# Expert choices of images 8 to 31 placed between the expert products, with fewer and wider casts of the score parts

## What is computed

```python
logits = jnp.einsum('bsd,ed->bse', x, gate_w)            # 64 experts
top_logits, indices = jax.lax.top_k(logits, 6)
scores = jax.nn.softmax(top_logits, axis=-1)
W_sel = lattice_weights[indices]                          # 64x64 each
xW = jnp.einsum('bsd,bskde->bske', x, W_sel)
lattice_out = jnp.einsum('bske,bsk->bse', xW, scores)
h = x + jnp.einsum('bsd,ed->bse', lattice_out, out_w) + out_b   # then a layernorm
```

## Time and profile before

| | us |
|---|---|
| median of 3 runs | 1178.67 (1178.66 to 1181.56) |
| the profiled execution | 1181.52 |
| its span, first to last instruction | 1179.7 |
| PE busy in it | 1075.1 (91%) |
| DVE, ACT, POOL busy | 625.6, 422.6, 125.5 |
| mean granted TensorE clock | 0.962 of full speed |

### The profile page before, as it was taken

The page is one execution under the profiler, slowest core; times in us unless marked ns, Lnnn a source line. Parts: engine busy times, 40 slices in busy tenths (PEclk is TensorE's granted clock), DMA queues, the critical chain, the costliest instruction groups (busy, mean ns, idle before and its releaser), DMA issues.

```text
span 1179.7 us, 34307 instructions
## 1 busy us (share of the span) xinstructions
PE 1075.1 (91%) x15860; PEld 715.5 (61%) x15860; DVE 625.6 (53%) x790; ACT 422.6 (36%) x588; POOL 125.5 (11%) x120
## 2 busy tenths in 40 slices
PE   5899999999999998999899999999998999349996
PEld 4578667767767533677677677767226888322221
DVE  2238445824834221358248446733153577857887
ACT  2332223133223485231332233223667786540000
POOL 6000000000000000000000000020012754242111
PEclk9999999999999899999999999999899999559998
DMA  5220130022022201300220130020001000000000
GB/s 179 86 72 2 50 97 13 2 86 72 3 71 76 83 6 63 82 19 2 86 72 2 64 88 8 2 93 9 13 15 38 2 1 2 1 1 1 5 5 10
DMA packets 25652, 46.62 MB, mean 40 GB/s; under 512 B 9437, under 2 KB 10488, under 8 KB 24869
## 3 DMA queue, kind: packets, MB, share of 16 engines
q1 hardware_dynamic: 24694, 43.49, 12.2%
q10 hardware_dynamic: 384, 0.66, 0.2%
q0 software_dynamic: 432, 0.29, 0.1%
HBM read 30.25 MB, written 10.89 MB: 35 GB/s over the span
## 4 chain that ended last, share of the span: by engine, by line
PE 77%; DVE 11%; ACT 4%; issue 2%; DMA 2%; SPq 1%; POOL 1%; ACTq 0%; POOLq 0%; DVEq 0%
PE PSALL L1198 22%; PE PSALL L1057 9%; PE PSALL L1166 7%; PE PSALL L1074 7%; PE PSALL L482 5%; DVE WORK L1390 5%; PE PSALL L1276 4%; PE PSALL L1189 4%; PE PSALL L1142 4%; PE PSALL L1286 3%; PE PSALL L470 2%; PE PSALL L387 2%; DMA WORK<-MIXED 2%; DVE WORK L1409 2%; PE PSALL L366 2%
## 5 line engine op out<-in xcount | busy, mean ns | idle before, releaser
L1409 DVE STREAM_TRANSPOSE WORK<-PSALL 128x1024 f32<-128x1024 f32 x128 | 152.4, 1229 | 320.2 <-PE PSALL L1166 320.2
L1198 PEld LDWEIGHTS PSALL<-EW,WORK 64*128 64x128 f32 x4096 | 251.5, 194 | 65.5 <-issue 48.3
L1198 PE MATMUL PSALL<-EW,WORK 64*128 64x128 f32 x4096 | 267.8, 284 | 12.8 <-DVE WORK L1409 12.8
L1326 ACT ACTIVATE X<-PSALL,TABLES 128x1024 f32<-128x1024 f32 x128 | 141.9, 1115 | 334.4 <-PE PSALL L1198 334.4
L1390 DVE STREAM_TRANSPOSE WORK<-PSALL 128x1024 f32<-128x1024 f32 x100 | 119.1, 1229 | 58.4 <-PE PSALL L1057 54.6
L1074 PE MATMUL PSALL<-TABLES,WORK 128*128 128x128 f32 x1000 | 138.9, 288 | 4.7 <-DVE WORK L1390 0.5
L1074 PEld LDWEIGHTS PSALL<-TABLES,WORK 128*128 128x128 f32 x1000 | 121.2, 195 | 32.7 <-issue 19.2
L1307 ACT COPY SPEC<-PSALL 128x400 f32<-128x400 f32 x64 | 53.7, 847 | 175.4 <-PE PSALL L1074 172.2
L1057 PE MATMUL PSALL<-WORK,DW 32*64 32x256 f32 x3200 | 103.4, 389 | 12.6 <-DMA B<-in_fc_b 12.6
L1386 DVE STREAM_TRANSPOSE WORK<-X 128x1024 f32<-128x1024 f32 x96 | 111.4, 1204 | 0.0
L932 DVE TENSOR_TENSOR WORK<-PSALL,X 128x832 f32<-128x832 f32 x80 | 80.7, 1021 | 19.7 <-PE PSALL L470 19.5
(11 more groups left out here) (145 smaller groups left out, 983.0 us busy)
## 6 DMA issues: line engine op xcount, KB each, us to landing
SW<-in_spec_w SPq DMA_DIRECT2D x160, 80.0 KB, 2.4
spec_scr<-MIXED SPq DMA_DIRECT2D x24, 400.0 KB, 3.3
SPEC<-spec_scr SPq DMA_DIRECT2D x32, 200.0 KB
WORK<-spec_scr SPq DMA_DIRECT2D x16, 200.0 KB
WORK<-MIXED SPq DMA_DIRECT2D x64, 40.0 KB
WORK<-in_coords_w SPq DMA_DIRECT2D x2, 1024.0 KB, 4.9
XC<-in_coords_c SPq DMA_DIRECT2D x2, 1024.0 KB, 7.1
hid_scr<-WORK SPq DMA_DIRECT2D x64, 8.0 KB
```

Of the source, the lines that this page charges most:

```text
L1198: m = pe.matmul(PS[2 * p + z][:, 2 * b * GRID:(2 * b + 2) * GRID], G[64 * z:64 * z + 64, n % 2, b, h:h + 4, :, c].rearrange("p q o -> p (q ...
L1326: nc.scalar.activation(X[:, n].rearrange("p b (z d) c w -> p d z b (c w)", z=2)[:, p, :, :, 2 * t * GRID:2 * (t + 1) * GRID], PSALL[:, 2 * ...
L1409: nc.vector.transpose(G[:, n % 2, 2 * x + y].rearrange("p h o v -> p o h v"), PSALL[:, 4 + 2 * x:6 + 2 * x, :].rearrange("p k (h o v) -> p ...
```

## The change

Only choice 0 (images 0 to 7) and the parts of chunks 0 and 1 stay in the step loop, which ends at i = 51. The gate rows of the last two chunks come at steps 48 and 50. Choices 1 to 3 start on DVE after the products of pairs 0, 10 and 20, one step per pair, and their remainders 10 and 12 pairs on; PE makes their score rows at pairs 9 and 11 on; ACT's exponentials and casts and POOL's products stand outside the step loop, in the order of the choices. The two halves of the experts share one instruction: one high cast of 96x520, one remainder and one middle cast of 64x520, one low part of 32x520. High, middle and low now lie in the third, second and first 32 rows. The score products are steps 7 and 8. `SC3` and the logits `LG` move to other memory, since `ZX` and `LT` of the experts lie where they were. POOL's two long additions follow the last low part as before. The six matmuls at L337, whose result nothing reads, are there in both kernels.

```diff
-TAIL_STEPS = PARTS_AT + LB * (LK - 1) + 7
+TAIL_STEPS = 52
+CHOICE_PAIR = [None, 0, 10, 20]
+def rows_step(i):
+    if i <= ROWS_AT + 5 * BC:
+        return (i - ROWS_AT) // BC if i >= ROWS_AT and (i - ROWS_AT) % BC == 0 else None
+    return 6 + (i - ROWS_AT - 22) // 2 if i in (ROWS_AT + 22, ROWS_AT + 24) else None
...
-        LG = modes_mem[0:TOK, NT:NT + NIMG * LW].rearrange("p (b e) -> p b e", b=NIMG)
+        LG = arena[0:TOK, 14272:14272 + NIMG * LW].rearrange("p (b e) -> p b e", b=NIMG)
...
-               for m in (modes_mem[0:TOK, 0:LB * 6 * EH], arena[0:TOK, 14432:14432 + LB * 6 * EH])]
+               for m in (arena[0:TOK, 10272:10272 + LB * 6 * EH], arena[0:TOK, 12352:12352 + LB * 6 * EH])]
...
     PE, score_rows
-                for g in range(2):
-                    pe.wait_ge(sc_ready, c * BC // LB + 1)
-                    if c:
-                        pe.wait_ge(rest_ready, 2 * c - 1 + g)
-                    transposes(c, lambda b: SC3[b // LB % 2][:, b % LB, g]..., 3 * EH, PS[6 + g], st_full)
+                pe.wait_ge(sc_ready, 2 * (c * BC // LB + 1))
+                if c:
+                    pe.wait_ge(rest_ready, c)
+                for i in range(BC):
+                    b = c * BC + i
+                    for g in range(2):
+                        m = pe.transpose(PS[6 + g][0:3 * EH, i * TOK:(i + 1) * TOK], SC3[b // LB % 2][:, b % LB, g]...)
+                m.then_inc(st_full, 1)
...
     PE, expert loop
+                for k in range(1, LK):
+                    if n // 2 - CHOICE_PAIR[k] in (9, 11):
+                        score_rows(2 * k + (n // 2 - CHOICE_PAIR[k]) // 11)
...
     ACT
-                for g in range(2):
-                    act.wait_ge(st_full, 2 * c + g + 1)
-                    nc.scalar.copy(PARTS3[g][0:3 * EH, c * CT:(c + 1) * CT], PS[6 + g][0:3 * EH, 0:CT]).then_inc(high_ready, 1)
+                act.wait_ge(st_full, c + 1)
+                nc.scalar.copy(PARTS3[0:3 * EH, :, t], PSALL[0:3 * EH, 6:8, 0:CT]).then_inc(high_ready, 1)
...
-                for g in range(2):
-                    act.wait_ge(rest_ready, 2 * c + g + 1)
-                    for r in (EH, 2 * EH):
-                        m = nc.scalar.copy(PARTS3[g][r:r + EH, ...], REST[g][r:r + EH, ...])
-                    m.then_inc(mid_ready, 1)
+                act.wait_ge(rest_ready, c + 1)
+                nc.scalar.copy(PARTS3[0:2 * EH, :, t], REST[0:2 * EH, :, t]).then_inc(mid_ready, 1)
...
+            exp_logits(1)
             for z in range(NZ):
+                for k in ([1], [2, 3])[z] if z < 2 else []:
+                    high_part(2 * k)
+                    middle_part(2 * k)
+                    high_part(2 * k + 1)
+                    if k + 1 < LK:
+                        exp_logits(k + 1)
+                    middle_part(2 * k + 1)
...
     POOL
+                nc.gpsimd.tensor_tensor(PARTS3[0:EH, :, t], REST[0:EH, :, t], PARTS3[0:EH, :, t], ALU.subtract).then_inc(lo_ready, 1)
...
+            for k in range(1, LK):
+                chosen_scores(k)
+                low_part(2 * k)
+                low_part(2 * k + 1)
...
     DVE, expert loop, after each product L932
+                    for k in range(1, LK):
+                        step = n // 2 - CHOICE_PAIR[k]
+                        if 0 <= step <= 8:
+                            choice(k, step)
+                        if step in (10, 12):
+                            rest(2 * k + step // 12)
```

More of the change, by code:

```diff
@@ L449, in tail_tensor @@
                     turn_attended((i - LAG - 2) // BC)
[L450 to L457, removed]
+                if rows_step(i - 1) is not None:
+                    gate_logits(rows_step(i - 1))
+                if rows_step(i) is not None:
+                    gate_rows(rows_step(i))
+                if i in (PARTS_AT, PARTS_AT + 2):
+                    score_rows((i - PARTS_AT) // 2)
             pe.wait_ge(gt_ready, NC)
@@ L489, in output_projection @@
                 if c == 0:
[L490 removed]
+                    pe.wait_ge(rest_ready, NC)
                 if c >= 2:
@@ L603, in tail_scalar @@
                     deviation(1, (i - LN_STEP - 7) // LB)
[L604 to L615, removed]
-            for z in range(NZ):
+                if rows_step(i - 1) is not None:
+                    gate_logits_out(rows_step(i - 1))
+                if rows_step(i) is not None:
+                    gate_rows_out(rows_step(i))
+                if i == CHOICE_AT + 2:
+                    exp_logits(0)
+                if i in (PARTS_AT, PARTS_AT + 2):
+                    high_part((i - PARTS_AT) // 2)
+                if i in (PARTS_AT + 3, PARTS_AT + 5):
+                    middle_part((i - PARTS_AT) // 4)
+            exp_logits(1)
+            for z in range(NZ):
+                for k in ([1], [2, 3])[z] if z < 2 else []:
[5 more added lines that the diff above has]
+                    middle_part(2 * k + 1)
                 if z >= 2:
@@ L647, in tail_pool @@
             for g in range(2):
-                nc.gpsimd.memset(PARTS3[g][3 * EH:128], 0.0).then_inc(zeros_set, 1)
+                nc.gpsimd.memset(PARTS3[3 * EH:128, g], 0.0).then_inc(zeros_set, 1)
                 pool.wait_ge(zeros_set, g + 1)
@@ L676, in low_part @@
             def low_part(c):
[L677 to L681, removed]
+                pool.wait_ge(weighed, c // 2 + 1)
+                t = slice(c * CT, (c + 1) * CT)
+                pool.wait_ge(mid_ready, c + 1)
+                nc.gpsimd.tensor_tensor(PARTS3[0:EH, :, t], REST[0:EH, :, t], PARTS3[0:EH, :, t], ALU.subtract).then_inc(lo_ready, 1)
             pool.wait_ge(nv_ready, NC)
@@ L707, in tail_pool @@
                     square(1, (i - LN_STEP - 3) // LB)
[L708 to L713, removed]
+                if i == CHOICE_AT + 5:
+                    chosen_scores(0)
+                if i in (PARTS_AT + 4, PARTS_AT + 6):
+                    low_part((i - PARTS_AT) // 6)
+            for k in range(1, LK):
+                chosen_scores(k)
+                low_part(2 * k)
+                low_part(2 * k + 1)
+            pool.wait_ge(lo_ready, NC)
             whole = [TOK, NIMG, GRID]
@@ L840, in choice @@
                         link(nc.vector.reciprocal(st[:, 3, a], st[:, 0, a]))
[L841 removed]
+                    if step in (7, 8):
                         if k >= 2:
[L843 to L848, removed]
+                            dve.wait_ge(st_full, LB // BC * (k - 1))
+                        g, thrice = step - 7, [TOK, LB, 3, EH]
+                        nc.vector.tensor_tensor(SC3[k % 2][:, :, g], SC[:, a, g * EH:(g + 1) * EH].unsqueeze(2).broadcast_to(thrice),
+                                                st[:, 3, a].unsqueeze(2).unsqueeze(3).broadcast_to(thrice), ALU.mult).then_inc(sc_ready, 1)
                 def rest(c):
                     t = slice(c * CT, (c + 1) * CT)
[L852 to L855, removed]
+                    dve.wait_ge(high_ready, c + 1)
+                    nc.vector.tensor_tensor(REST[0:2 * EH, :, t], PSALL[0:2 * EH, 6:8, 0:CT], PARTS3[0:2 * EH, :, t], ALU.subtract
+                                            ).then_inc(rest_ready, 1)
                 for i in range(TAIL_STEPS):
[L858 to L860 removed]
                     if i < NIMG:
@@ L902, in tail @@
                                                     ).then_inc(half_ready if step == 1 else y_ready, 1)
[L903 to L908, removed]
+                    if i == CHOICE_AT - 1:
+                        dve.wait_ge(ho_out.sem, PASSES * ho_out.stride)
+                        link(nc.vector.memset(LG[:, :, EXPERTS:LW], SENTINEL))
+                    if CHOICE_AT <= i <= CHOICE_AT + 8:
+                        choice(0, i - CHOICE_AT)
+                    if i in (PARTS_AT + 2, PARTS_AT + 4):
+                        rest((i - PARTS_AT) // 4)
                 def add_projection(c):
```

18 lines of the change are left out of this document (10 added, 8 removed).

## The result

The kernel after takes 1165.26 us (median of 4 runs, 1163.19 to 1167.91) against 1178.66 (4 runs, 1177.11 to 1181.56): ratio 0.9903, 95% interval 0.9874 to 0.9932. The profiled execution took 1165.57 us, its span is 1163.8. Timed again (6 runs, beside 11 of the kernel before) it gave 1166.65 against 1176.02, ratio 0.9930 (0.9903 to 0.9957). Forecast were 1171.7 and a gain of 7.0 us; the gain is 13.4 us by the first set and 9.4 by the second.

A forecast was written before the change was run, and what follows sets the result against it. Ahead of the experts a chain hopping between engines, none full, was taken as the bound, then PE in the experts. -27.8 + 14.2 + 2.6 + 4.0 = -7.0 us takes the median from 1178.67 to 1171.7; range 1165 to 1181.

The forecast's parts named there:

- Start of the experts, -27.8: Chain ahead of the experts: with three choices gone from it, the first expert product comes at 1026.4 against 1054.2 us.
- Pairs 0 to 32, +14.2: Expert pairs with choice steps on DVE's queue: DVE becomes the bound, 59.0 us against 44.8, a loss of 14.2.
- the added 1.7: Pairs 0 to 32: 1.7 us for half clock at the start, waits after score products and a meeting with POOL.
- POOL's additions, +2.6: POOL's two long additions move behind pair 32; DVE waits 3.7 us and PE loses about 2.6.
- PE runs on for about one pair of its ring: During DVE's wait for POOL after product 37, PE keeps working about one pair, so it loses about 2.6 us.
- the bound of 3.7: Upper bound of the loss from POOL's additions: DVE's whole wait after product 37, 3.7 us.
- TensorE's clock, +4.0: Pairs 0 to 32: two or three falls of PE's clock, costing 4 us.
- The crowded pairs should cost a fall each: Pairs 10 to 12 and 20 to 22, PE about 60% busy: each a clock fall of about 6 us.
- The sum without the clock: Whole change without the clock term: -27.8 for the start, +14.2 for the pairs, +2.6 for POOL's additions.
- Rival 1: Clock holds in pairs 0 to 32, PE's gaps under 1 us each; the 4 us fall away, 1167.7; chance 0.22.
- Rivals 2 and 3: Pairs 0 to 32: clock at each level half the time, 1176.7, chance 0.18; clock stays 0.50, 1194, chance 0.12.

The follow-up runs named there:

- the run with the held low parts: Kernel after with POOL's last residual shift started after choice 1's subtraction, and low parts of chunks 0 and 1 held until DVE's normalizations are done: 1159.89 us.
- the narrow run: Kernel after with two high casts, four middle casts, two remainders and two low parts per chunk again: 1170.27 us, ratio 0.9940.
- the padded one: Kernel after with one unused DVE maximum over 65x512 behind each of products 0 to 31; products 0 to 33 took 77.86 us, single profiled run.
- the run with only the wide casts: Kernel after with all four choices back ahead of the experts, wide casts, joined remainders and low parts kept: 1175.69 us against 1176.86, ratio 0.9993.

## Why the prediction was right

The time lies in the range and the direction is right; the mechanism was as forecast: experts early, DVE the bound for 33 pairs, POOL's additions uncovered. By its steps:

- **Start of the experts, -27.8.** Measured 41.94 to 14.68, -27.3 (with product 0, -27.4). The middle cast, 0.62 us, was priced at 0.60. Missing was that POOL's low parts would hold up DVE's normalizations (3.05 us for two, PE idle 1.40), which the run with the held low parts puts at 0.9.
- **Pairs 0 to 32, +14.2.** Measured +12.6. The sum of DVE's instructions was 57.3 and the stretch took 57.43, but that they meet is partly luck: DVE was busy 55.2 us of it and idle 2.2. Waits of about the size of the added 1.7 were there, and the terms for the instructions, taken from start to start, were 2 too high.
- **POOL's additions, +2.6.** Measured +3.9, and 4.4 by the run that moves one of them away. The step that failed is "PE runs on for about one pair of its ring": the bound of 3.7, the whole wait, was nearly the price. PE, the bound from there on, gets nothing back; it idled 3.11 us in one piece and then ran at half clock for 3 us in one execution and some 7 in the other.
- **TensorE's clock, +4.0.** Measured 0. This is the term that was mis-sized, and the reason that the gain is larger than forecast. "The crowded pairs should cost a fall each" failed twice. At 2.49 us of work in 4 the clock held in both crowded places (from 1044 and from 1062), and it held from product 2 to product 33 in seven of the eight profiles with this stretch unpadded; and a fall costs little there, half a microsecond or less in the narrow run and 1.4 to 3.6 us for three in the padded one, because DVE has the longer queue. I carried the fall in the earlier trace rows over from a place with other matmuls.
- **The sum without the clock**, -11.0, lies near the -10.75 of the trace because three smaller errors nearly cancel: the start gained 0.5 less, the pairs lost 1.6 less, POOL's additions cost 1.3 more. That closeness is luck too.
- Rival 1 (the clock holds) is what happened, although PE's gaps were not all under 1 us, as it had them: they go up to 1.28. Rivals 2 and 3 need a half clock over much of the stretch; no run had that with the stretch unpadded, so their prices stay untested. The rule of the Trainium skill (TensorE: Matmul & The Clock Gate, "A second HAM failure mode: psum-queue depth-cycling") that short idles between groups of matmuls can make the clock go back and forth isn't borne out by the kernel after, where gaps of 0.15 to 1.28 us at 43.87 us of work in 54 left the clock at 1.00. In the padded run, where PE had 1.37 us of work in 4, it went down and up three times, as the page says.
- The rest of the 13.4 us in the medians, some 2.2, is not shown to belong to the change. In the later sets the kernel before had medians of 1176.86 (23 runs), 1176.02 and 1175.64 (11 each), so the first set's 1178.66 lay high; the second pair of timings is 9.4 us apart, and the change is worth 10.2 to 11.2 by the traces, the 0.4 in front included.

What stays open: why the clock fell in one run after PE had worked 2.58 of 4 us and held in another after 2.49 of 4. Nothing here tells these two apart. Nor is it shown where the 0.4 us ahead of the score rows come from; the run with only the wide casts has them too (14.92).

## What to carry to other kernels

A chain of short steps that hops between engines costs its whole length; put between the units of a stage with slack on the chain's main engine it costs only what overfills that engine, here 12.6 us for three choices that had put 27.4 us ahead of the first product. When it is moved, look at what followed it on the other queues: POOL's two additions lost their cover and cost about 4 us, and moving one of them helped only at a place where DVE wasn't reading two SBUF operands. Compare stages between instructions that both traces have, not spans.

## What the runs showed that was not expected

- One instruction where there were two gained nothing on a chain that was pipelined by halves (1175.69 against 1176.86), although ACT's casts went from 2.5 to 1.2 us per chunk. In the new placement the same instructions were worth 3.7 us.
- DVE instructions with both operands in SBUF grew by about what POOL did beside them: two took 1.29 us with POOL quiet, 3.05 beside the low parts, 7.65 beside these and the long addition.
- Two executions of the same code had score rows 3.64 us apart; the later one had two falls of the clock in the head (near 407 and 472) that the other lacks.
